# The second turning of x through the contexts' bank at the end of step 6, the second weighing at the end of step 7: what it does to an attention loop

## The reference, cut to what matters

```
h = concat([cls_tok, tok(x)], axis=1)               # 32 x 129 x 1024
h = h + attn(layernorm(h), Wq, Wk, Wv, Wo)          # 32 heads of 32, 8 key heads, causal, rotary
h = h + ffn(layernorm(h), w, b)                     # weights and rows rounded to 8 bits
```

## Time and profile before

| what | value |
| --- | --- |
| median of 3 runs | 1506.73 us (1504.13 to 1507.42) |
| the profiled execution's own time | 1501.35 us |
| its span, from the first to the last instruction | 1499.6 us |
| mean granted clock of TensorE | 0.980 |
| busy: PE, DVE, POOL, ACT | 95%, 80%, 56%, 49% |
| chain that ended last: PE | 82% |
| of it projection matmuls of the attention (L1097) | 35% |
| waits for ScalarE's exponentials: ACT pr L1225 on DVE ml L1400 | 155.6 us in all |

### The profile page before, as it was taken

One profiled execution on the slowest core, in us unless ns is written; L12 is line 12 of the kernel. 1 busy time (PEld: TensorE's weight loads), 2 busy tenths in 40 slices (PEclk: granted clock), 3 DMA queues, 4 the chain that ended last, 5 costly groups with the idle time before them and its releaser, 6 DMA issues.

```text
span 1499.6 us, 34041 instructions
## 1 busy us (share of the span) xinstructions
PE 1427.6 (95%) x10442; PEld 1111.9 (74%) x10442; DVE 1196.9 (80%) x2349; ACT 733.8 (49%) x2673; POOL 838.7 (56%) x894
## 2 busy tenths in 40 slices
PE   5999889999999999999999999769999999999997
PEld 3999867777777777777777777556777777777774
DVE  7888678889999999998999999676866666666665
ACT  6897566666766767676676767551000000000000
POOL 5796156667676767667676767422433334334342
PEclk8999999999999999999999999879999999999998
DMA  9356666667777777777767766865444344443441
GB/s 238 97 143 151 190 141 180 181 190 212 210 195 210 194 200 202 200 202 204 212 192 209 194 200 187 265 204 152 133 129 142 106 143 121 123 146 106 140 119 53
DMA packets 263402, 255.60 MB, mean 170 GB/s; under 512 B 73297, under 2 KB 201554, under 8 KB 263346
## 3 DMA queue, kind: packets, MB, share of 16 engines
q1 hardware_dynamic: 257586, 233.87, 56.2%
q10 hardware_dynamic: 5760, 21.04, 4.6%
HBM read 138.26 MB, written 106.57 MB: 163 GB/s over the span
## 4 chain that ended last, share of the span: by engine, by line
PE 82%; DVE 5%; POOL 5%; DMA 3%; issue 2%; ACT 1%; SPq 1%; ACTq 0%; DVEq 0%; POOLq 0%
PE att_ps L1097 35%; PE ffn_o L1703 23%; PE ffn_y L1794 8%; PE att_ps L1140 5%; PE att_ps L1152 4%; POOL yb L358 3%; PE att_ps L1129 2%; PE att_ps L1121 2%; POOL yb L364 2%; DMA p_blocks<-pB 1%; PE mix_ps L447 1%; PE att_ps L1108 1%; SPq L877 1%; DVE m L641 1%; DVE kb L542 1%
## 5 line engine op out<-in xcount | busy, mean ns | idle before, releaser
L1225 ACT ACTIVATE pr<-sm,ml 128x128 f32<-128x128 f32 x1024 | 399.1, 392 | 155.6 <-DVE ml L1400 155.6
L980 POOL TENSOR_TENSOR pr<-pr,ri 128x512 f32<-128x512 f32 x256 | 266.3, 1040 | 213.3 <-DVE ri L1407 206.0
L1097 PE MATMUL att_ps<-w_lo,xT_hi 128*128 128x512 f32 x776 | 319.6, 412 | 0.0
L1097 PE MATMUL att_ps<-w_hi,xT_hi 128*128 128x512 f32 x776 | 312.4, 403 | 4.4 <-DVE xT_lo L1348 3.6
L1097 PE MATMUL att_ps<-w_hi,xT_lo 128*128 128x512 f32 x776 | 307.4, 396 | 0.0
L1749 ACT CAST cT_hi<-ctx_in 128x512 fp32r<-128x512 f32 x64 | 36.4, 616 | 370.3 <-PE ffn_o L1703 360.8
L1703 PE MATMUL ffn_o<-wo_hi,cT_hi 128*128 128x512 f32 x528 | 212.5, 402 | 2.6 <-ACT wo_hi L1733 2.5
L1391 DVE TENSOR_TENSOR sm<-att_ps,cst 128x512 f32<-128x512 f32 x256 | 169.9, 664 | 52.3 <-PE att_ps L1140 52.3
L1703 PE MATMUL ffn_o<-wo_hi,cT_lo 128*128 128x512 f32 x528 | 206.6, 391 | 0.0
L1703 PE MATMUL ffn_o<-wo_lo,cT_hi 128*128 128x512 f32 x528 | 206.0, 390 | 0.0
L1225 ACT ACTIVATION_READ_ACCUMULATOR pr<-sm,ml 128x1 f32 x1024 | 193.4, 189 | 0.0
(11 more groups left out here) (207 smaller groups left out, 2396.1 us busy)
## 6 DMA issues: line engine op xcount, KB each, us to landing
pT<-p_blocks SPq DMA_DIRECT2D x256, 256.0 KB, 2.9
p_blocks<-pB SPq DMA_DIRECT2D x512, 64.0 KB, 2.0
h_rows<-ho SPq DMA_DIRECT2D x64, 256.0 KB, 3.7
ctx_turned<-ctxo SPq DMA_DIRECT2D x64, 256.0 KB, 3.2
h_in<-h_rows SPq DMA_DIRECT2D x32, 512.0 KB, 3.6
out_dram<-yo SPq DMA_DIRECT2D x32, 512.0 KB, 2.7
ctx_in<-ctx_turned SPq DMA_DIRECT2D x30, 512.0 KB, 3.6
hbuf<-h_rows ACTq DMA_DIRECT2D x29, 512.0 KB, 4.7
```

The costliest lines, as they stand in the source:

```text
L980: G.tensor_tensor(pr[:, g % 4], pr[:, g % 4], ri[:, g % 2, :].unsqueeze(2).to_broadcast([P, GQ, P]), ALU.mult).then_inc(p_ready, 1)
L1097: mm = nc.tensor.matmul(bank[:], x_part[:, t[1], e, tok:tok + P], w_part[blk][:, e, :], start=(r == 0), stop=(r == EC * 3 - 1))
L1225: a = nc.scalar.activation(pr[:, g % 4, q, :], sm[:, g % 2, q, :], ACT.Exp, bias=ml[:, b[1], 0, h:h + 1], accum_out=ml[:, b[1], 1, h:h + 1])
```

## The change

What it does, engine by engine, for the tiles of the loop:
- TensorE: `turn_x(n, 1)` writes C_BANK for every tile, and stands at the end of step 6 instead of the middle of step 7. It waits for the low halves of the tile before, not for the first half of its own, and for the copy of the contexts' first half. `weigh(c, 1)` stands at the end of step 7, behind the 5 projection matmuls, and waits for the low half of the second turning.
- ScalarE: `context(c, 1)` stands behind the exponentials of step 7 instead of ahead of them. `split_x(n, 1)` keeps its place at the start of step 7.
- VectorE: `split_x(n, 1)` stands right behind `split_x(n, 0)`, ahead of the mask of step 7, instead of at the step's end.
- SP: the store of the second contexts goes to step 0 of the next iteration, behind that step's `part_p` and `whole_p`; the last tile's stays in step 7.
- GpSimd: its order is not changed.

```diff
--- before.py
+++ after.py
@@ -773,7 +773,7 @@
 
     def x_bank(n, r):
 
-        return C_BANK if r == 1 and fixed(n) and nth(n) <= 2 else Y_BANK
+        return C_BANK if r == 1 else Y_BANK
 
     def heads_of(g):
 
@@ -799,7 +799,7 @@
 
     def x_steps(n):
 
-        return (3, 4) if at(n, 0) else (6, 7)
+        return (3, 4) if at(n, 0) else (6, 7) if last_rows(n) else (6, None)
 
     def wo_rounds_at(t, s):
 
@@ -927,7 +927,9 @@
                     whole_p(d, g)
                 if s == 1 and exists(c, NB):
                     store_ml(c)
-                if s == 7 and exists(c, NB):
+                if s == 0 and exists(shifted(t, -3), NB):
+                    store(shifted(t, -3), 1)
+                if s == 7 and at(t, NB + 1):
                     store(c, 1)
             if at(t, NB):
                 load_scales(sp)
@@ -1123,8 +1125,10 @@
 
         def turn_x(n, r):
             pe.wait_ge(xn_ready, XROUNDS * nth(n) + r + 1)
-            at_least(pe, x_lo, 2 * nth(n) + (r if x_bank(n, r) is Y_BANK else 0))
+            at_least(pe, x_lo, 2 * nth(n))
             at_least(pe, k_stored, number(n))
+            if r == 1 and exists(shifted(n, -3), NB):
+                pe.wait_ge(ctx_ready, 2 * number(shifted(n, -3)) + 1)
             for q in range(4):
                 mm = nc.tensor.transpose(x_bank(n, r)[:, q * P:(q + 1) * P],
                                          xn[:, (4 * r + q) * P:(4 * r + q + 1) * P], ident)
@@ -1146,6 +1150,8 @@
             pe.wait_ge(p_whole[half], 64 * (u + 1))
             pe.wait_ge(v_moved, u + 1)
             at_least(pe, ctx_ready, 2 * u + half)
+            if half == 1 and exists(shifted(b, 3), NB):
+                pe.wait_ge(x_lo, 2 * nth(shifted(b, 3)) + 2)
             for j in range(4):
                 g = 4 * half + j
                 for q in range(GQ):
@@ -1176,12 +1182,14 @@
                 for r in range(XROUNDS):
                     if s == x_steps(n)[r] and has_rows(n):
                         turn_x(n, r)
-                if s == 7 and exists(c, NB):
-                    weigh(c, 1)
                 for r in rounds_at(t, s):
                     pe_round(pe, r)
                 if has_rows(t):
                     project(t, min(s * per_step + ahead, count), min((s + 1) * per_step, count))
+                if s == 6 and has_rows(n) and x_steps(n)[1] is None:
+                    turn_x(n, 1)
+                if s == 7 and exists(c, NB):
+                    weigh(c, 1)
                 if at(t, NB):
                     if s == 0:
                         pe.wait_ge(rot_ready, NBLK * (NB + 1))
@@ -1289,10 +1297,8 @@
                 if s == 5 and exists(t, NB):
                     store_k(t)
                 for r in range(XROUNDS):
-                    if s == x_steps(n)[r] and has_rows(n):
+                    if s == (x_steps(n)[r] or 7) and has_rows(n):
                         split_x(n, r)
-                if s == 7 and exists(c, NB):
-                    context(c, 1)
                 for r in rounds_at(t, s):
                     act_round(act, r)
                 for u in w_quantise_at(t, s):
@@ -1300,6 +1306,8 @@
                 d, g = group_at(t, s, 1)
                 if exists(d, NB):
                     exponentials(d, g)
+                if s == 7 and exists(c, NB):
+                    context(c, 1)
 
         iterations(act, body)
 
@@ -1426,8 +1434,10 @@
                 d, g = group_at(t, s, 4)
                 if exists(d, NB):
                     part_turned(d, g)
-                if s == x_steps(n)[1] and has_rows(n):
+                if s == (x_steps(n)[1] or 7) and has_rows(n):
                     split_x(n, 0)
+                    if x_steps(n)[1] is None:
+                        split_x(n, 1)
                 d, g = group_at(t, s, 1)
                 if exists(d, NB):
                     mask(d, g)
```

## The result

| what | before | after |
| --- | --- | --- |
| median, in one comparison | 1505.78 us (4 runs, 1504.13 to 1507.42) | 1493.49 us (4 runs, 1491.5 to 1494.69) |
| ratio, with its 95% interval | | 0.9917 (0.99 to 0.9934) |
| profiled execution: own time, span | 1501.35, 1499.6 us | 1494.69, 1492.9 us |
| mean granted clock of TensorE | 0.980 | 0.975 |

The change makes the kernel faster by 12.3 us, 0.8%. The forecast was 8.2 us and 1498.5 us; 1493.49 lies at the very end of the range (1493.5), outside it by 0.01.

The account below looks back on a forecast made before the run. TensorE, busy 95% of the span, was taken to pace the loop. 26 iterations x 0.24 = 6.2 us plus 2.0 us from early iterations gave 8.2 us, so 1506.7 - 8.2 = 1498.5 us, range 1493.5 to 1506.5.

Parts of the forecast that it names:

- the 0.51: TensorE's interval from last projection to second turning before the change; forecast to become one plain interval, 0.24 us.
- The price of projection to weighing: On TensorE, the weighing starts 0.33 us after a projection, taken from projection to scores; bounds 0.24 and 0.44.
- The chain over mask, exponentials, contexts and q: From VectorE's mask over ScalarE's exponentials and copies to the scores: q ends at 578.94, scores at 579.05 against 579.25.
- GpSimd makes VectorE's mask late: GpSimd's late save_ctx and normalisation delay VectorE's next mask some 0.45 us, hidden by its wait for scores.
- VectorE's wait for GpSimd: VectorE's transposition of step 1 waits 0.6 to 0.7 us for GpSimd's late softmax normalisation.
- SP's store: On SP's queue the second contexts' store goes behind one part_p and one whole_p; costed at nothing.
- the choice of 0.24 us for an iteration, between 0.20 and 0.30: Gain per repeating iteration: 0.20 if q's copy decides, 0.30 if TensorE does; 0.24 taken, 6.2 us over 26.
- TensorE's own sum: TensorE's matmul intervals up to the scores, without waiting for q: there at 578.95, 0.30 us won.
- the rival that was given 0.12: TensorE alone decides: 26 x 0.32 + 2.5 = 10.8 us gained, 1495.9 us; chance 0.12.
- Early iterations, 2.0 us: In three early iterations with late VectorE, scores come 0.84 us sooner each, 2.5 in all; 2.0 taken.
- wait moves to the scores: Rival: TensorE waits at the scores instead of the turning; gain 0 to 2.5 us, 1504.2 to 1506.7; chance 0.16.
- GpSimd sets VectorE's pace: Rival: late save_ctx delays normalisation, transposition and mask; with 0.5 us over, 1511 us; chance 0.14.

Follow-up runs that it names:

- e5: The changed kernel with x's second subtraction back at the end of VectorE's step 7, behind mask and row maximum: 1513.49 us, ratio 1.0054 to before.
- e6: The changed kernel with GpSimd's save_ctx(c, 1) put behind the softmax normalisation of the next step 0: 1495.37 us, ratio 0.9926 to before.
- e4: The changed kernel with ScalarE's context(c, 1) ahead of the exponentials of step 7 again: 1493.3 us, ratio 0.9922 to before.
- e3: The kernel before with only VectorE's first subtraction moved to the very start of step 7: 1491.62 us, ratio 0.9917 to before.
- e8: The changed kernel with the second turning back in the middle of step 7, still in C_BANK: 1506.59 us, ratio 0.9999 to before.
- e13: One more trace of the kernel before, without an edit: own time 1504.23 us.

## Why the prediction was right or wrong

**Right.** What bounds the loop: TensorE, and 0.58 us added before the weighing reached the scores whole (e5). What the change takes away: the 0.51 is 0.23. The price of projection to weighing, which no row showed: 0.33, as taken. The weighing isn't kept waiting in a repeating iteration: the low half ends at 616.92, 0.26 ahead of it (forecast: 0.3). The chain over mask, exponentials, contexts and q holds to 0.1 us (table above). GpSimd makes VectorE's mask late: it starts 1.83 after the scores (620.92 to 622.75), where before it was 1.34 (579.25 to 580.59), so 0.49 late, forecast 0.45; and that stays hidden (e6). VectorE's wait for GpSimd in front of it is 0.42, where 0.6 to 0.7 was forecast. SP's store was costed at nothing; no run takes it alone.

**Wrong: the choice of 0.24 us for an iteration, between 0.20 and 0.30.** The prediction held that the copy of q decides and that TensorE waits for it. Two terms of the chain were taken from the nearest rows and are too long here: the exponentials follow the row maximum's start by 0.72 (617.55 to 618.27), not 0.80; the scores follow the end of q's copy by 0.05 (620.87 to 620.92), not 0.11, and it is 0.05 in e4 too (621.05 to 621.10), where they do wait for it. So the chain ends at 7.96 instead of 8.11, at the same moment as TensorE's own sum (forecast 8.01), which e3 gives as 7.96 with q out of the way. TensorE's own work sets the pace, and q is in time without a margin that can be seen. That is the rival that was given 0.12. Its price was 0.32 an iteration. Measured are 8.305 less 7.98 = 0.325 as means from first turning to scores, and 0.03 to 0.04 more between those scores and the scores of step 5 (11.34 in before, 11.30 after), which stays unexplained; e3 lacks it. 26 x 0.36 = 9.4 us instead of 6.2.

**Early iterations, 2.0 us.** Measured are 3.7 over the first six, of which one regular 0.36 is to be taken off: 3.3. This isn't all the forecast mechanism. Against the three traces of before with a granted clock of 0.99 in that stretch (mean 153.1) the change's 151.4 is 1.7 less, or 1.3 without the regular 0.36, somewhat under the forecast. The other 2.0 come from the three traces of before with more half clock, which the prediction did not have and did not price. Whether the change makes these stretches rarer, or its four traces happened to miss them, stays open. The step's mechanism is seen: the wait moves from the turning to the weighing (5.5 to 3.4 us), and from the third early iteration on the scores stand 0.40 to 0.46 after a projection, as they do in e4, where they wait for q. e3's kernel took 151.5 us twice in that stretch.

**Where the missing 5.0 us are.** The forecast was 1498.5, the result 1493.49. The loop gave 3.2 us more than summed, the early iterations 1.3. Another 0.95 is the starting point: the forecast went from 1506.73, and before's median in the comparison is 1505.78. These make 5.4; the 0.4 over is within the scatter. The range ended at 1493.5: TensorE alone with 0.32 for 26 iterations and 2.5 us for the early ones (1495.9), and 2.4 more for a cheaper change of the tile shape, which did not come (0.33, as taken). So even the right mechanism at its forecast price would have been 2.4 us above the result.

**Wrong as well: the distance from the profiled execution to the median.** It was kept at 5.4 us. The median forecast doesn't hang on it, since the 8.2 us were taken off the median, but the profiled execution's own time does: forecast 1493.2, measured 1494.69. That execution of before was a quick one: 1501.35, where all 67 runs of before in this study have a mean of 1505.6 (1497.6 to 1512.0, standard deviation 2.6). After the change the median was 1.2 below the profiled one. The loop doesn't scatter (24.05 to 24.08); the start, the early iterations and the rest do.

**The sum as measured:** -8.7 (24 iterations), -3.7 (early six), +1.9 (start), +0.8 (rest) = -9.7 us between the means of the traces, and -12.3, -11.5 and -11.2 between medians. The start, where nothing was changed in the order of work, and the rest scatter by about as much as they differ: e3's kernel, traced twice, took 199.0 and 202.5 us at the start. Six traces with that deviation don't fix a mean to better than 1 us either way; whether the remaining 2 us are scatter or something in the executions that no trace caught stays open.

The rivals: *wait moves to the scores* did not happen in the loop, though e4 shows that the margin was next to nothing; *GpSimd sets VectorE's pace* is refuted by e6. A longer iteration than before came only when x's second low half was late, by VectorE's order (e5, 24.28) or by the turning's place (e8, 24.23). The prediction had that point as covered by 0.3 us in the change, and it is.

## What to carry to other kernels

Where an engine waits for a shared bank, look first at what the releasing engine does just ahead of its release: one subtraction moved in front of a transposition (e3) gave all that a rearrangement over four engines gave. When two chains end within 0.1 us of each other, as q's and TensorE's own did here, prices from the nearest rows can't tell which decides: two of them were too long by 0.06 to 0.08 us. Forecast both outcomes, and don't give either a small chance. And read more than one execution by stage, with the granted clock of each stage, before one profile is taken for the kernel: here the loop repeated to 0.03 us an iteration and the early stretch moved by 6 us, up to 3 of them with the clock.

## What the runs showed of the hardware

A stall costs a little more than its length: with the turning held, the weighing came 0.56 after it; with no stall (e3) 0.53. A pair of matmuls with a change of the tile shape between them stands further apart than one without: by about 0.10 us behind a 128x512 matmul (0.33 against 0.23), and by about 0.17 behind a turning that wasn't held (0.53 against 0.36 to a projection). The first weight load of the new shape also starts together with its matmul (both at 617.18 at the weighing, both at 620.92 at the scores), while a projection's starts 0.23 ahead of it (616.62, matmul at 616.85). The Trainium skill, TensorEngine Tiling (Array Packing), Key Properties, says that changing the mode drains the array. The traces agree that there is a price, and show that it depends on what stands in front; no run here tells a drain from the later weight load.

ScalarE took up an exponential 0.72 us after the row maximum that releases it had started, in another place 0.80, with the same shapes on both sides. At a granted clock of 0.50 the 32 matmuls of a weighing took 1.94 us (e13, at 282.08), at 1.00 they take 1.08.
